# A routed layer of MLP and spline experts: the second spline layer with stationary weights, its sums copied and transposed back, and the block counts of the plain tiles read ahead

## What is computed

```python
h   = gelu(x @ mlp_W1 + mlp_b1);  mlp_out = h @ mlp_W2 + mlp_b2          # 128 -> 512 -> 128
h0  = layernorm(x) * g0 + b0
z   = basis(h0) @ kan_sl_W0 + kan_sl_b0                                  # 128*8 -> 256
h1  = layernorm(z) * g1 + b1
kan_out = basis(h1) @ kan_sl_W1 + kan_sl_b1                              # 256*8 -> 128
basis(x)[g] = 1 - tanh((x - grid[g]) / 2)**2,   g in 0..7
out = x1 + sum over the two chosen experts of weight * expert_out
```

## Time and profile before

| | |
|---|---|
| median of 3 runs | 927.51 us |
| range | 927.06 to 932.16 us |
| the profiled execution | 928.66 us |
| its span | 926.8 us |
| mean granted TensorE clock | 0.925 |

### The profile page before, as it was taken

The page is one execution under the profiler, slowest core; times in us unless marked ns, Lnnn a source line. Parts: engine busy times, 40 slices in busy tenths (PEclk is TensorE's granted clock), DMA queues, the critical chain, the costliest instruction groups (busy, mean ns, idle before and its releaser), DMA issues.

```text
span 926.8 us, 20634 instructions
## 1 busy us (share of the span) xinstructions
PE 765.3 (83%) x7113; PEld 571.6 (62%) x7114; DVE 465.0 (50%) x1076; ACT 533.1 (58%) x697; POOL 491.9 (53%) x699
## 2 busy tenths in 40 slices
PE   4599979799798797988945857999999999999870
PEld 2246555465454554546513645888988898889770
DVE  6525516355163362643501664565867785787330
ACT  4477756567475575666714626366677666766410
POOL 8334536545265254651572347548677767764431
PEclk9799989989899898999966979899999999999975
DMA  2330402204013040030162316255456446443213
GB/s 60 114 99 2 123 12 64 71 2 125 10 46 88 2 122 13 34 101 2 42 100 50 131 15 165 47 138 132 72 150 155 112 94 147 131 73 61 22 17 106
DMA packets 93698, 70.72 MB, mean 76 GB/s; under 512 B 41602, under 2 KB 85922, under 8 KB 91684
## 3 DMA queue, kind: packets, MB, share of 16 engines
q1 hardware_dynamic: 76660, 57.74, 22.0%
q0 software_dynamic: 16912, 11.35, 8.9%
HBM read 49.51 MB, written 21.36 MB: 76 GB/s over the span
## 4 chain that ended last, share of the span: by engine, by line
PE 59%; ACT 11%; DVE 9%; issue 9%; POOL 4%; another core or an unknown queue 4%; DMA 1%; SPq 0%; DVEq 0%; ACTq 0%; POOLq 0%
PE pv L1542 12%; PE ring L1509 12%; PE pv L1629 10%; ACT Pb L927 4%; PE ring L1601 4%; PE ring L1588 4%; PE ring L1475 3%; PE ring L1493 3%; ACT Pb L936 2%; DVE maxima L1185 2%; PE ring L1688 2%; DVE h L1237 2%; PE ring L1569 2%; PE ring L1428 1%
## 5 line engine op out<-in xcount | busy, mean ns | idle before, releaser
L927 ACT ACTIVATE Pb<-ring 128x1024 f32<-128x1024 f32 x160 | 156.5, 1025 | 64.6 <-PE ring L1588 62.8
L766 POOL TENSOR_SCALAR_AFFINE_SELECT Pb<-Pb 128x512 f32<-128x512 f32 x128 | 79.3, 637 | 208.7 <-ACT Pb L927 208.7
L745 POOL DMA_INDIRECT acc_d<-stack,srec x84 | 138.2, 1645 | 69.9 <-issue 35.8
L1629 PE MATMUL pv<-Pb,vaug 128*32 128x192 f32 (+4 forms) x2048 | 138.1, 399 | 18.3 <-issue 15.9
L936 ACT ACTIVATE Pb<-ring 128x768 f32<-128x768 f32 (+1 forms) x128 | 89.7, 759 | 98.1 <-remote 61.0
L1118 DVE SCALAR_TENSOR_TENSOR stack<-stack 128x512 f32<-128x512 f32 x160 | 103.3, 689 | 72.4 <-ACT stack L905 38.1
L1509 PE MATMUL ring<-stack 128*128 128x256 f32 x560 | 126.5, 383 | 8.4 <-issue 8.3
L1509 PEld LDWEIGHTS ring<-stack 128*128 128x128 f32 x560 | 106.0, 191 | 26.7 <-issue 12.4
L1629 PEld LDWEIGHTS pv<-Pb,vaug 128*32 128x32 f32 x2048 | 65.9, 117 | 82.0 <-issue 58.8
L905 ACT ACTIVATE stack<-ring,kprm 128x512 f32<-128x512 f32 x160 | 108.1, 814 | 0.1
L1588 PE MATMUL ring<-stack 128*128 128x128 f16 (+3 forms) x512 | 90.5, 306 | 18.0 <-issue 10.7
(11 more groups left out here) (232 smaller groups left out, 1171.3 us busy)
## 6 DMA issues: line engine op xcount, KB each, us to landing
stack<-L_ffn_kan_sl_W SPq DMA_DIRECT2D x20, 1024.0 KB
stack<-hl_d SPq DMA_DIRECT2D x24, 256.0 KB
stack<-hl_d SPq DMA_DIRECT2D x24, 128.0 KB
stack<-L_ffn_mlp_W SPq DMA_DIRECT2D x12, 256.0 KB
hl_d<-hi SPq DMA_DIRECT2D x7, 384.0 KB, 2.6
hl_d<-lo SPq DMA_DIRECT2D x7, 384.0 KB, 3.3
Pb<-L_ffn_mlp_W SPq DMA_DIRECT2D x10, 256.0 KB
xb<-L_attn_x SPq DMA_DIRECT2D x9, 256.0 KB
```

The costliest lines, as they stand in the source:

```text
L745: pool.indirect_dma_start(acc_d, bass.IndirectOffsetOnAxis(ap=srec[:, kind, u % RECS, q, 0:1], axis=0), src[:, u % 2, q, :], None, compute ...
L766: pool.affine_select(pd, pd, [[0, HG], [1, P]], ALU.is_ge, 0.0, base=0, channel_multiplier=-1).then_inc(pd_ready, 1)
L927: act.activation(Pb[:, n % 2, at:at + 1024].rearrange("p (k q) -> p k q", k=2), slot(job), ACT.Square, bias=1.0).then_inc(freed[job % SLOT ...
L1629: mm = pe.matmul(pv[32 * j:32 * (j + 1), n // 2 % 2, P * c:P * c + w], vaug[:, p, c, head(n, j) // 2, 16 * (n % 2):16 * (n % 2) + 32], src ...
```

## The change

`kan_second` swaps its operands: a 128x128 piece of the weights is stationary and 256 rows of the basis functions move, 16 matmuls for each half tile (the upper half is left out where the count is two or less; a tile of three blocks computes the whole upper half). The sums now stand with the features on the partitions. So `result_copied` (DVE) copies them to a new buffer `k_yd` in SBUF and adds the bias, which is now one number per partition (bias times -1/4, a 28th column of the parameters); `result_turned` (PE) transposes the four blocks back into the same PSUM bank; `result_weighted` (DVE) multiplies by -4 and the gate weight in one operation. The load of the bias per tile is gone.

PE's `mlp_first(u+2, parts 0, 1)` now stands between `kan_second(u)` and `result_turned(u)` (for tile 1 ahead of the loop) rather than at the start of the next turn. `load_blocks(0, ...)` is read once a tile, before `kan_second`, and handed to `mlp_first` and `mlp_second`, which read it themselves before. Each part of `mlp_first` waits for its own gelu only.

```diff
@@ set-up @@
-        kp_raw = sb("kp_raw", [P, E2, 6])
-        kp_all = sb("kp_all", [P, E2, 27])
+        kp_raw = sb("kp_raw", [P, E2, 7])
+        kp_all = sb("kp_all", [P, E2, 28])
-        kprm = sb("kprm", [P, RECS, 27])
+        kprm = sb("kprm", [P, RECS, 28])
...
+            with nc.allow_non_contiguous_dma(reason="512 words"):
+                sp.dma_start(kp_raw[:, :, 6], kb1.rearrange("e p -> p e")).then_inc(kp_loaded, 16)
...
                 sp.wait_ge(k_y, tile_no(k, back=2))
                 sp.dma_start(w[:, 2048:4096].rearrange("p (f x) -> p f x", f=2),
                              kW1[e].rearrange("a (f p g) n -> (a p) f (g n)", f=2, g=G)).then_inc(k_w1[u % 2], 16)
-                sp.dma_start(k_bias1[u % 2], kb1[e].to_broadcast([P, D])).then_inc(k_w1[u % 2], 16)
...
-            dve.wait_ge(kp_loaded, 16 * 7)
+            dve.wait_ge(kp_loaded, 16 * 8)
+                dve.tensor_scalar(kp_all[:, e, 27:28], kp_raw[:, e, 6:7], -0.25, None, ALU.mult)
...
                 dve.wait_ge(m_h, tile_no(k, F // P, back=1))
                 dve.tensor_copy(mxs, m_banks[0]).then_inc(m_xs, 1)
 
-            def weighted(kind, i, u):
-
-                k = i * UNROLL + u
-                rec_sem, added, mm_sem, dst, y_sem, y, bias, bias_sem = (
-                    (m_srec, m_added, m_mm, m_res, m_y, m_banks[1], m_bias, m_w2),
-                    (k_srec, k_added, k_mm[1], k_res, k_y, pv[:, 1, :], k_bias1, k_w1))[kind]
-                dve.wait_ge(rec_sem[u % RECS], use_no(RECS, i, u, 16))
-                dve.wait_ge(bias_sem[u % 2], use_no(2, i, u, 32))
-                dve.wait_ge(added, tile_no(k, back=2))
-                dve.wait_ge(mm_sem, tile_no(k))
+            def weighted(i, u):
+
+                k = i * UNROLL + u
+                dve.wait_ge(m_srec[u % RECS], use_no(RECS, i, u, 16))
+                dve.wait_ge(m_w2[u % 2], use_no(2, i, u, 32))
+                dve.wait_ge(m_added, tile_no(k, back=2))
+                dve.wait_ge(m_mm, tile_no(k))
                 full = [P, Q4, D]
-                dve.scalar_tensor_tensor(dst[:, u % 2], y.rearrange("p (q d) -> p q d", d=D), (1.0, -4.0)[kind],
-                                         bias[u % 2].unsqueeze(1).to_broadcast(full), ALU.mult, ALU.add
-                                         ).then_inc(w_sum[kind], 1)
-                dve.wait_ge(w_sum[kind], tile_no(k))
-                dve.tensor_tensor(dst[:, u % 2], dst[:, u % 2], weight[:, kind, u % RECS, :, 1:2].to_broadcast(full),
-                                  ALU.mult).then_inc(y_sem, 1)
+                dve.tensor_tensor(m_res[:, u % 2], m_banks[1].rearrange("p (q d) -> p q d", d=D),
+                                  m_bias[u % 2].unsqueeze(1).to_broadcast(full), ALU.add).then_inc(m_sum, 1)
+                dve.wait_ge(m_sum, tile_no(k))
+                dve.tensor_tensor(m_res[:, u % 2], m_res[:, u % 2],
+                                  weight[:, 0, u % RECS, :, 1:2].to_broadcast(full), ALU.mult).then_inc(m_y, 1)
+
+            def result_copied(i, u):
+
+                k = i * UNROLL + u
+                dve.wait_ge(k_w0[u % 2], use_no(2, i, u, 48))
+                dve.wait_ge(k_mm[1], tile_no(k))
+                dve.tensor_scalar(k_yd, pv[:, 1, :], kprm[:, u % RECS, 27:28], None, ALU.add).then_inc(k_yc, 1)
+
+            def result_weighted(i, u):
+
+                k = i * UNROLL + u
+                dve.wait_ge(k_srec[u % RECS], use_no(RECS, i, u, 16))
+                dve.wait_ge(k_added, tile_no(k, back=2))
+                dve.wait_ge(k_yT, tile_no(k))
+                dve.scalar_tensor_tensor(k_res[:, u % 2], pv[:, 1, :].rearrange("p (q d) -> p q d", d=D), -4.0,
+                                         weight[:, 1, u % RECS, :, 1:2].to_broadcast([P, Q4, D]), ALU.mult, ALU.mult
+                                         ).then_inc(k_y, 1)
 
             def basis_functions(z, i, u, steps=None):
 
...
                         with dve.If(k + 1 < n_kind[1]):
                             hidden_stats(i, u + 1)
                         with dve.If(k + 1 < n_kind[0]):
-                            weighted(0, i, u + 1)
+                            weighted(i, u + 1)
                         with dve.If(k + 2 < n_kind[1]):
                             basis_functions(0, i, u + 2)
                         with dve.If(k + 1 < n_kind[1]):
                             hidden_norm(i, u + 1)
                         with dve.If(k < n_kind[1]):
-                            weighted(1, i, u)
+                            result_copied(i, u)
+                            result_weighted(i, u)
 
 
         @blk.tensor
...
                 products(0)
                 products(1).then_inc(done, 1)
 
-            def mlp_first(i, u, parts=range(F // P)):
+            def mlp_first(i, u, blocks, parts=range(F // P)):
                 k = i * UNROLL + u
                 pe.wait_ge(m_w1[u % 2], use_no(2, i, u, 32))
                 pe.wait_ge(m_xs, tile_no(k))
                 pe.wait_ge(m_y, tile_no(k, back=1))
-                if parts[-1] > 1:
-                    pe.wait_ge(m_g, tile_no(k, F // P, parts[-1] - 1))
                 half = TS // 2
 
                 def products(f, at):
+                    if f > 1:
+                        pe.wait_ge(m_g, tile_no(k, F // P, f - 1))
                     return pe.matmul(m_banks[(f + 1) % 2][:, at:at + half], mw[u % 2][:, P * f:P * (f + 1)],
                                      mxs[:, at:at + half], start=True, stop=True)
 
-                with pe.If(load_blocks(0, k) > 2):
+                with pe.If(blocks > 2):
                     for f in parts:
                         products(f, half)
                 for f in parts:
                     products(f, 0).then_inc(m_h, 1)
 
-            def mlp_second(i, u):
-                k = i * UNROLL + u
-                blocks = load_blocks(0, k)
+            def mlp_second(i, u, blocks):
+                k = i * UNROLL + u
                 pe.wait_ge(m_w2[u % 2], use_no(2, i, u, 32))
                 pe.wait_ge(m_g, tile_no(k, F // P, F // P - 1))
 
...
             def kan_second(i, u):
                 k = i * UNROLL + u
                 blocks = load_blocks(1, k)
-                pe.wait_ge(k_w1[u % 2], use_no(2, i, u, 32))
+                pe.wait_ge(k_w1[u % 2], use_no(2, i, u, 16))
                 pe.wait_ge(k_y, tile_no(k, back=1))
 
-                def products(q):
+                def products(at, n):
                     for g in range(2 * G):
                         pe.wait_ge(k_bas[1], tile_no(k, 2 * G, g + 1))
-                        mm = pe.matmul(pv[:, 1, P * q:P * (q + 1)], basis[1][g][:, P * q:P * (q + 1)],
-                                       kw[u % 2][:, 2048 + D * g:2048 + D * (g + 1)], start=(g == 0),
-                                       stop=(g == 2 * G - 1), skip_group_check=True)
+                        mm = pe.matmul(pv[:, 1, at:at + n], kw[u % 2][:, 2048 + D * g:2048 + D * (g + 1)],
+                                       basis[1][g][:, at:at + n], start=(g == 0), stop=(g == 2 * G - 1),
+                                       skip_group_check=True)
                     return mm
 
-                for_blocks(blocks, products, k_mm[1])
+                with pe.If(blocks > 2):
+                    products(TS // 2, TS // 2)
+                products(0, TS // 2).then_inc(k_mm[1], 1)
+
+            def result_turned(i, u):
+                k = i * UNROLL + u
+                pe.wait_ge(k_yc, tile_no(k))
+                for q in range(Q4):
+                    mm = pe.transpose(pv[:, 1, P * q:P * (q + 1)], k_yd[:, P * q:P * (q + 1)], identf[:])
+                mm.then_inc(k_yT, 1)
 
             def batches():
                 for s, n, j, b in PROGRAM:
...
                     if s == "erows" and n > 0:
                         rows_transposed(2 - n, 0, 1)
                     if s == "ehid":
-                        mlp_first(0, 0, [n])
+                        if n == 0:
+                            pe.wait_ge(first_ready, 1)
+                            m_blocks = load_blocks(0, 0)
+                        mlp_first(0, 0, m_blocks, [n])
                     if s == "efirst" and n == 3:
...
 
 
             n_kind = load_counts(pe)
+            m_blocks = load_blocks(0, 1)
+            with pe.If(n_kind[0] > 1):
+                mlp_first(0, 1, m_blocks, range(0, 2))
             with pe.Fori(0, TURNS) as i:
                 with pe.If(i * UNROLL < n_kind[2]):
                     for u in range(UNROLL):
                         k = i * UNROLL + u
-                        with pe.If(k + 1 < n_kind[0]):
-                            mlp_first(i, u + 1, range(0, 2))
+                        if u == 0:
+                            m_blocks = load_blocks(0, k + 1)
                         with pe.If(k < n_kind[1]):
                             hidden_transposed(i, u)
                         with pe.If(k + 1 < n_kind[0]):
```

(28 more changed lines are left out.)

## The result

The changed kernel takes 924.95 us (median of 20 runs, 919.38 to 928.39) where the kernel before took 929.32 (20 runs beside them): ratio 0.9949, interval 0.9929 to 0.9969, so 4.7 us less. The profiled execution took 919.62 us at a span of 917.8, one of the fastest, and that of before (928.66) was near its median; so the 9.0 us between the two profiles say twice what the runs say.

The account below looks back on a forecast made before the run. Matmuls in PE's program order were taken to bound the expert stage. Terms of +1.9, +4.0, +1.9, -9.6, -1.3 and -4.0 summed to -7.1 us, giving a forecast of 920.4 us, range 916 to 927.

Parts of the forecast that it names:

- Terms 1 and 2: Second spline layer, before the last tile: 1, matmuls with swapped operands, +1.9 us; 2, transposing back in nine tiles, +4.0.
- The spacing rule: Skill page: load and matmul both set spacing; would put a full second-layer tile at 8.6 us, term 1 at about -42.
- weight loads: Rival: weight loads bound the second layer, saving up to 7.1 us in each of seven tiles, under 880; chance 0.02.
- Term 3: Copy out of PSUM before transposing back: mostly covered by moved `mlp_first` half, +1.9 us; uncovered 0.9 a turn.
- Term 4: Idle stretch before the second half of `mlp_first`: count read early and finer wait remove it, -9.6 us.
- branch, not load: Rival: the branch, not the count's load, makes the idle gap; term 4 halves, 925.2 us; chance 0.14.
- load, not wait: Term 4's upper bound: all 10.6 us of idle before `mlp_first`'s second half go if the count's load was the gap.
- Term 5: Ahead of the expert loop: gaps of 0.9 and 0.37 us around count reads go, -1.3 us.
- Term 6: Last tile: fewer products left after its last basis function, full clock, earlier last scatter behind the MLP's, -4.0 us.
- The front gains are swallowed: Rival: PE's instruction wait at 571.9 to 583.0 ends with POOL's gathers, losing earlier gains; 922.7 us; chance 0.08.
- second stretch of missing instructions: Rival: another stretch of PE waiting for instructions falls where PE bounds, costing 7.6 us (928.0) or more; chance 0.10.
- DVE's queue in the way: Rival: DVE's queue holds the copy behind `hidden_norm` in four more turns, +5.6 us, 926; chance 0.08.

Follow-up runs that it names:

- e5: The changed kernel, but a tile of three blocks computes only three blocks in the second spline layer; ratio to the kernel before 0.9905 (850.38 against 860.23 us).
- e6: The changed kernel with `result_turned` ahead of the next tile's `mlp_first`, so no matmuls cover the copy; ratio to the kernel before 1.0140.
- e1: The kernel before with only the block counts read ahead, once a tile in front of `kan_second`; old wait and old second layer kept; ratio 0.9926.
- e2: The kernel before with only the wait changed: each part of `mlp_first` waits for its own gelu, behind load and branch, counts read in place; ratio 0.9895.
- e8: The kernel before with the fine wait and the old second spline layer taking two blocks beside each other, one start per pair; ratio 0.9915.
- e11: The same kernel as e8 measured again, on one chip with the fine wait alone and the changed kernel; 853.73 us, ratio to the kernel before 0.9935.
- e12: The changed kernel itself measured again on another chip; 854.06 us, ratio to the kernel before 0.9940.
- e7: The changed kernel with the counts read where they are used, each part of `mlp_first` still waiting for its own gelu; ratio to the kernel before 0.9973.
- The pairs: Kernel before with the fine wait and the old second spline layer multiplying two blocks beside each other per basis function; ratios 0.9915 (e8) and 0.9935 (e11).
- e4: The kernel before with counts ahead, fine wait and two blocks beside each other, start set for both blocks of a pair, omitting a sum term; ratio 0.9921.

## Why the prediction was right, term by term

It said 920.4 us and faster. It was faster by 4.7 us [2.9, 6.6] where 7.1 had been forecast: the mechanisms were right, the sizes of three terms were not, and part of the gain lies where the runs do not show it.

- **Terms 1 and 2** (+1.9, +4.0 = +5.9): about +4.8 by starts; the busy time in the turns is 3.4 more. Term 1 took 14.08 for a full tile from a row's length, which has the whole modelled end of its last record in it; by starts it is 13.91 (64 x 0.217 us), so a full tile gains 0.38, not 0.21, and a tile of two blocks 0.14. The third tile's fourth block cost 3.2 by starts (+3.4 forecast), and e5 has 2.7 to 2.8 of it back. Term 1 is +0.6, term 2 +4.2 (0.44 to 0.49 a tile). The spacing rule weighed in the prediction does not hold here (0.217 us a record of 256 columns, 0.112 of 128); weight loads were no bound.
- **Term 3** (+1.9): 0.6 in the turns with a small MLP tile, +1.05 at tiles 5 and 8 by starts: 1.7. That the whole cover is worth 0.9 a turn was wrong: e6 shows 1.3 to 1.75, and 3.6 in the two turns where the clock fell.
- **Term 4** (-9.6, the gap of 1.09 in each turn): by starts the gap was 0.70 to 1.38, and it is gone everywhere. The residue stands elsewhere than I said, ahead of `kan_second`, where the moved load now is: 0.1 to 0.4 a turn, 1.8 in all, for 1.0. Waiting in the nine turns fell by 5.6 with term 3's price in it. My account of the cause was half right. The rival "branch, not load" is out (e1), and so is my own version "load, not wait": e2 keeps both in place and removes most of it.
- **Term 5** (-1.3): both gaps are gone. The 0.93 ahead of the loop is not there (550.96 follows L1106 directly), nor the 0.37. In the runs this is under the spread of the front.
- **Term 6** (-4.0): products end 7.7 after the last basis function (forecast 7.4), the clock stays at 1.00, `k_y` comes after 9.96 (9.8). But the scatter gains 2.5, not 4.0. I let the MLP's scatter land 2.1 us after its issue (894.85 to 897), and its last packet does end 2.07 after; but I let the next scatter start at that moment, and it starts 3.7 after the issue (2.95 to 3.9 in e8, e11, e12 and e7). Where the landing itself is recorded, in e7 and e8, it comes 2.87 and 1.95 after the issue, and the next scatter starts 1.0 us behind it. What failed is a hand-over put at nothing.

The sum, by place: of the 7.1, 2.3 lay ahead of the first `kan_second` (term 5 and 1.0 of term 4) and 4.8 behind it. Behind it the profiles give 5.1 and 5.2. That this part agrees so well is luck in part: terms 1 and 2 came 1.1 cheaper, and some of the kernel before's own waits inside its products (0.9) went too, while the last scatter gave 1.5 less and the residue took 0.8 more. The 2.3 of the front are what the whole lacks: the runs give 4.7 in all, no more than the loop alone.

Of the rivals one is not refuted. *The front gains are swallowed* said 922.7, so 4.8 less, the number nearest to the measured one. In the two profiles nothing is swallowed: PE starts the first layer of tile 1 2.5 us earlier and the second layer of tile 0 3.4 us earlier, and the stretch at 572 stayed (PE 4.68 of 11.10 us busy, 3.45 before). But the profiles' front spreads by 7 us, so it stays open. No second stretch of missing instructions fell into the turns, no further turn had DVE's queue in the way, and weight loads did not bound.

The larger finding is what the new layer is for. The fine wait, two lines, gives -5.5 to -5.9 by turns and tail; all the rest of the change adds nothing to it, since the layer's 3.4 us of work and 1.8 of waiting pay for the 2 to 3 us of tail. With e5's branch it gives -7.9 by turns and tail, 2 us more; by the runs this can't be told from the fine wait alone (0.9905 against 0.9895 and 0.9948).

## What to carry to other kernels

In this kernel a register load and a branch cost about a microsecond (0.70 to 1.38 us a turn) where they stood behind a semaphore wait at which PE had run out of work, and 0 to 0.6 where they were read while matmuls still ran: put the load ahead of the wait, and let each piece of work wait only for what it needs. Price a wait that you are about to uncover by everything that follows it, the granted clock too, not by the wait alone. Where a kernel ends in a chain through a scatter, shortening the arithmetic ahead stops paying at the landing of the transfer before and its hand-over.

## What was not expected

**Two chips, 70 us apart, for one kernel.** The same changed kernel took 924.95 and 854.06 us. Its turns and tail are alike (274.6 + 31.8 and 274.4 + 31.9); the first `kan_second` started at 586.1 on one and 524.7 us on the other, which is all of the 61 us between the two profiles. 52.5 of them lie ahead of the first layer of tile 1 (557.17 and 504.63). In the attention part of the slower one ACT waits again and again, up to 11.2 us at a time, for what the profile can't name; the other chip has the same row with a fifth of the time:

```profile
ACT Pb L938 <- remote: 57.9, 22, 11.2
ACT Pb L938 <- remote: 10.9, 4, 3.3
```

The mean granted clock was 0.929 and 0.948. What the waits are, the profile doesn't show. The other 8.9 us are the stretch at 572: from the first layer of tile 1 to the first `kan_second` it is 28.9 us on one chip and 20.1 on the other, whose trace has no such row of single PE records 2 us apart. That PE waited for its own instructions there is not shown: the DMA records have transfers of 8 KB of instructions 2.1 us apart at its start (569.80, 571.89 and 574.04 in the kernel before, with single PE records at 573.00, 575.13 and 577.27), which fits and no more. An absolute time carries nothing from chip to chip here; ratios beside the kernel before do, and a count from inside the loop does best.

**A skipped branch that costs 2 us.** The pairs' first tile of two blocks, above (2.13 and 2.57 us in e8 and e11; 0.62 and 1.01 there in e4), while the second such tile shows none. A transfer of 16 KB of instructions is recorded at each (652.65 to 653.58 in e8, 659.11 to 660.04 in e11, 716.97 to 718.01 in e4); the fine wait alone has one at the same place (721.80 to 722.78) and no standstill. The cause stays open.
